# Adding slots on VectorE before TensorE sums them, in every group of a graph network kernel

## The reference, cut to what matters

```python
N_NODES, E, D = 6250, 200000, 16        # edges sorted by dst
w_m = (efeat @ W_msg + b_msg).reshape(E, 16, 16)
w_a = (efeat @ W_attn + b_attn).reshape(E, 16, 16)
h_src = feat[src][:, :, None]
e1, e2 = w_m * h_src, w_a * h_src
ex = exp(e2 - segment_max(e2, dst)[dst])
attn = ex / segment_sum(ex, dst)[dst]
ft = segment_sum(e1 * attn, dst).sum(axis=1)
x = layernorm(x + ft)
x = layernorm(x + segment_sum(edge_attr, dst) / max(counts, 1))
```

## Time and profile before

| | us |
|---|---|
| median of 3 runs | 2246.91 (2246.26 to 2247.14) |
| span of the profiled execution | 2950.2 |
| PE busy in it | 2137.9 |
| DVE busy | 1862.0 |
| POOL busy | 1687.5 |
| ACT busy | 1256.9 |
| mean granted TensorE clock | 0.861 |

### The profile page before, as it was taken

The page is one execution under the profiler, slowest core; times in us unless marked ns, Lnnn a source line. Parts: engine busy times, 40 slices in busy tenths (PEclk is TensorE's granted clock), DMA queues, the critical chain, the costliest instruction groups (busy, mean ns, idle before and its releaser), DMA issues. The chain is left out here.

```text
span 2950.2 us, 21765 instructions
## 1 busy us (share of the span) xinstructions
PE 2137.9 (72%) x6682; PEld 952.6 (32%) x6682; DVE 1862.0 (63%) x2907; ACT 1256.9 (43%) x1228; POOL 1687.5 (57%) x1845
## 2 busy tenths in 40 slices
PE   2347676676877777877787658877787767887777
PEld 1213233232333333333333223333333323333333
DVE  6246465566666666666676547766667656786776
ACT  3223443434444443454454325444444444554444
POOL 6556355665655565555565465655656565655633
PEclk8658888897988888989888889988989888988988
DMA  6000000000000000000000000000000001001000
GB/s 229 16 10 11 8 12 10 10 10 9 10 9 9 14 10 9 10 14 10 10 13 9 9 10 13 10 12 9 10 12 9 12 9 28 12 8 16 8 2 3
DMA packets 60073, 47.60 MB, mean 16 GB/s; under 512 B 28366, under 2 KB 55439, under 8 KB 59436
## 3 DMA queue, kind: packets, MB, share of 16 engines
q0 software_dynamic: 57632, 29.73, 8.0%
q1 hardware_dynamic: 2316, 16.38, 1.5%
HBM read 44.00 MB, written 1.90 MB: 16 GB/s over the span
## 5 line engine op out<-in xcount | busy, mean ns | idle before, releaser
L652 POOL DMA_INDIRECT AR<-in_xt,AR x1607 | 1538.8, 958 | 974.1 <-DVE AR L1472 491.3
L1128 PE MATMUL PX<-AR,CS 128*128 128x512 f32 x3246 | 1663.7, 642 | 37.8 <-issue 23.9
L1472 DVE CUSTOM_DVE_ANT_1 AR<-PW,AR 128x1024 f32<-128x1024 f32 x815 | 979.6, 1221 | 896.8 <-remote 651.2
L1108 PE MATMUL PW<-WS,LT 100*128 100x512 bf16 x1630 | 549.1, 423 | 683.9 <-DVE AR L1472 511.8
L1128 PEld LDWEIGHTS PX<-AR,CS 128*128 128x128 f32 x3246 | 664.9, 206 | 652.1 <-issue 532.4
L888 ACT ACTIVATE LT<-PTB 100x1024 bf16<-100x1024 bf16 (+1 forms) x221 | 211.2, 956 | 1005.7 <-remote 601.0
L1485 DVE TENSOR_TENSOR AR<-AR,PX 128x1024 f32<-128x1024 f32 (+1 forms) x442 | 501.0, 1134 | 121.3 <-ACT PX L944 76.0
L1108 PEld LDWEIGHTS PW<-WS,LT 100*128 100x128 bf16 x1630 | 141.5, 103 | 1113.7 <-DVE AR L1472 543.2
L946 ACT ACTIVATE AR<-AR 128x2048 f32<-128x2048 f32 (+1 forms) x221 | 412.9, 1869 | 7.2
L950 ACT ACTIVATE PX<-AR 128x1024 f32<-128x1024 f32 (+1 forms) x221 | 212.4, 961 | 412.3 <-DVE AR L1485 294.8
L944 ACT ACTIVATE PX<-AR 128x1024 f32<-128x1024 f32 (+1 forms) x221 | 231.0, 1045 | 39.4 <-DVE AR L1485 30.1
(11 more groups left out here) (192 smaller groups left out, 517.7 us busy)
## 6 DMA issues: line engine op xcount, KB each, us to landing
AR<-in_xt,AR POOLq DMA_INDIRECT x1607
AR<-in_eat SPq DMA_DIRECT2D x3, 3128.0 KB
AR<-in_eat SPq DMA_DIRECT2D x1, 3120.0 KB
y_d<-AR SPq DMA_DIRECT2D x1, 784.0 KB
AR<-y_d SPq DMA_DIRECT2D x1, 784.0 KB
AR<-in_es,E0I POOLq DMA_INDIRECT x48
y_d<-AR POOLq DMA_INDIRECT x36
CS<-in_cst SPq DMA_DIRECT2D x1, 442.0 KB, 5.3
```

What stands on the lines that cost most here:

```text
L652: g.indirect_dma_start(feat(h, j - j0, j - j0 + 1), None, xt, bass.IndirectOffsetOnAxis(ap=node, axis=0)).then_inc(hg_sem(h), 16)
L1108: i = pe.matmul(PAIRS[s % 2][:, j, :], LT[:, g % 3, lo:lo + 128], WS[:, :], start=True, stop=True)
L1128: i = pe.matmul(PDR, IDN, x, start=(a == 0 and j == 0), stop=(g == LAST[k] and j == n - 1))
L1472: v.tensor_tensor_reduce(em(g, j, j + 2).rearrange("p (x c) -> p x c", c=32), w, hb, 1.0, LOW, ALU.mult, ALU.max, accum_out=MXC[:, k % 2, ...
```

## The change

The list of groups whose slots VectorE adds first becomes all 221 groups:

```diff
 NORMS = [p for p, c in STEPS].index(FIRST[MAIN + 4] + 2)
-ADDS = [c for p, c in STEPS[-8:] if p is None]
+ADDS = list(range(NGR))
```

## The result

The changed kernel takes 2323.28 us (2322.32 to 2325.28, four runs), the kernel before 2246.59 (2244.28 to 2247.14, four runs): the ratio is 1.035, with a 95% interval of 1.0335 to 1.0364. The forecast was 2325.

What follows compares the result with a forecast made beforehand. GpSimd's gathers were taken as the bound: 2232 us plus 82 of holding gives 2314, against VectorE's 2255; with the leftover 2314 to 2329. Forecast 2325 us, 3.5% slower, range 2252 to 2352.

Steps and rivals of the forecast that it cites:

- The bound before: GpSimd's queue of gathers bounds the kernel before; its chain sums to 2232 us against the timed median of 2246.9.
- The missing 15 us: Part of the median before that GpSimd's sum left unexplained (0.7%); forecast to stay or shrink after the change.
- Part 1: TensorE sums fewer slots: 315 us less work, from 1843 to about 1528, off the path if GpSimd is the bound.
- Part 2: VectorE's new adds: 253 us more, 2025 us between first and last multiply; with 43 us for other waits, VectorE alone 2255.
- Part 4: Gathers starting inside an SBUF-and-SBUF add are held until it ends, less 0.12 us: 82 us more on GpSimd.
- lower bound of 46 us: Least price of the adds holding gathers, scaling the trace's 22 us of lengthening by add length and GpSimd's working share.
- The sum: GpSimd's chain 2232 + 82 = 2314 us against VectorE's 2255; with the leftover 2314 to 2329, forecast 2325, 3.5% slower.
- The first rival: Adds don't hold the gathers and VectorE is the bound: 2255 us (2225 to 2300); chance 0.17.
- The second rival: Timed runs are bound by TensorE handing pairs to VectorE, not by GpSimd: 2238 us; chance 0.06.
- The third: Gathers' hold-ups fall into GpSimd's waits for the ring, some 80 us free; VectorE still fits: 2247 us; chance 0.05.
- The fourth: Both effects plus a lower TensorE clock, VectorE and GpSimd waiting for each other: 2345 to 2380 us; chance 0.04.
- the signs listed: Gathers about 1000 ns or more, lengthened under L1493; 217 more adds; L1128 down a quarter; VectorE's L1108 waits shrink.

Runs made afterwards that it cites:

- b0_again: The kernel before, unchanged, run for a second trace because its first profiled span was 703 us too long: 2249.9 us (one run).
- b1: The kernel before with 213 of 1607 gathers left out (first slot of each group, columns 1 to 47): 2155.9 us, ratio 0.961.
- p1: The kernel before, all gathers, TensorE summing six of eight (five of six) slots, no new VectorE adds: 2245.5 us, ratio 1.0011.
- c2: The changed kernel with 213 gathers left out and TensorE still summing all slots, VectorE's adds kept: 2303.7 us, ratio 1.0238.
- p2: The changed kernel, all gathers and all adds, TensorE still summing all eight (six) slots: 2315.6 us, ratio 1.0323.
- a1: The changed kernel with 213 of 1607 gathers left out: 2305.8 us, ratio 1.0278 to the kernel before.
- h1: The changed kernel with the add in only every second group and the last four, all gathers: 2283.9 us, ratio 1.0158.
- h2: As the half-of-the-groups kernel, but its new adds replaced by a tensor_scalar with one SBUF input, 936 or 424 elements: 2250.2 us, ratio 1.0005.
- a2: The changed kernel with the 217 new adds replaced by a tensor_scalar with one SBUF input: 2321.2 us, ratio 1.0343.

## Why the prediction was right, and where it wasn't

**The bound before: right.** The forecast took GpSimd's gathers as the bound from a sum (2232 us), against a trace in which they weren't. b0_again shows VectorE waiting for gathers and never the other way, b1 gains 87 us by leaving gathers out, p1 gains nothing from a lighter TensorE. Setting the unnamed waits of the earlier trace rows aside, and adding up durations and spacings, was the right way to read a disturbed trace. The sum had one error that hid another: in undisturbed runs the steady gathers start at 73.8 us, not at 91.6, and the stretch behind the last gather is longer than 58 us. In b0_again the last gather starts at 2166.98, where the sum had 2174, and the end is 81 us later:

```profile
2166.98 0.94 POOL L652 DMA_INDIRECT AR<-in_xt,AR  x1 [0.30 <-issue]
```

The missing 15 us that the forecast carried along lie there: from the last gather to the last weights multiply it is 27 us, where the sum had 8. VectorE had fallen behind the gathers in the last columns, where it no longer waits for them.

**Part 1, TensorE's relief: right that it is off the path.** Its size was not: TensorE was to fall by 315 us and fell from 1965.8 to 1770.8, by 195. The same records got longer:

```profile
L1128 PE MATMUL PX<-AR,CS 128*128 128x512 f32 x3246 | 1553.5, 605 | 6.5 <-ACT AR L894 6.3
```

```profile
L1128 PE MATMUL PX<-AR,CS 128*128 128x512 f32 x2514 | 1306.2, 645 | 2.3 <-ACT AR L894 2.3
```

(before, second trace, then after: 605 and 645 ns). The mean granted clock went from 0.949 to 0.895. One place in the changed kernel where both show, TensorE and then VectorE:

```profile
331.15 0.60 PE L1108 MATMUL PW<-WS,LT 100*128 100x512 bf16 x2
334.95 1.03 PE L1108 MATMUL PW<-WS,LT 100*128 100x512 bf16 x2 [3.21 <-DVE AR L1472]
335.78 3.62 PE L1128 MATMUL PX<-AR,CS 128*128 128x512 f32 x4
339.19 1.06 PE L1108 MATMUL PW<-WS,LT 100*128 100x512 bf16 x2
```

```profile
338.23 0.08 DVE L1472 DVE_READ_ACCUMULATOR2_ANT AR<- 128x1 f32 x1
340.29 1.23 DVE L1472 CUSTOM_DVE_ANT_1 AR<-PW,AR 128x1024 f32<-128x1024 f32 x1 [1.98 <-PE PW L1108]
```

TensorE waits 3.21 us for VectorE (a product over the column's data, L1448, and the division and reduction, L1504 to L1506, stand before its next multiply) and comes back at a lower granted clock: 0.97 of full from 327.0 to 331.7 us, 0.88 from there to 334.95 and 0.50 from 334.95 to 339.2. Its weights product takes 1.03 us there, where the last one before the wait took 0.60. Its two slots then take 3.4 us until the next product, where they took 1.72 in the earlier trace rows, and VectorE stands for 1.98 us. So VectorE, though the bound, keeps losing time to the engine that waits for it. With a busier TensorE, in c2 and p2 (86% of the span in both, against 77% in a1 and 76% in the changed kernel), its mean clock is 0.950 and 0.946 (against 0.900 and 0.895) and the time is 0.1 to 0.4% better although it has more to do. What VectorE waits for before its weights multiplies is the same in sum, a1 then c2:

```profile
L1472 DVE CUSTOM_DVE_ANT_1 AR<-PW,AR 128x1024 f32<-128x1024 f32 x815 | 969.6, 1218 | 94.8 <-PE PW L1108 90.8 <-PE PX L1128 2.8 <-issue 0.4
...
L1473 DVE CUSTOM_DVE_ANT_1 AR<-PW,AR 128x1024 f32<-128x1024 f32 x815 | 969.1, 1219 | 93.3 <-PE PW L1109 66.7 <-issue 15.5 <-PE PX L1129 10.1
```

So less work at a lower clock and more work at a higher one hold VectorE up equally. What the clock costs by itself no run shows, since none changes the one without the other.

**Part 2, VectorE's work: the term that was mis-sized.** The forecast gave VectorE alone 2255 us. a1 measures 2306. The adds were right: 253 us forecast; measured were 215 more busy (1761 to 1976 between first and last multiply) and 23 of waiting right before them. The start was 22 us earlier than the disturbed trace had it. What failed is the idle time beside them, which I put at 64 us (21 for ScalarE, and 43, between 13 and 88, for TensorE's part and the filling). In a1 it is 185 us; less the 23 just named, 162. The waits for TensorE's products are the largest part, 91 us, then come 53 for ScalarE's exponentials before L1485, where the forecast had 21:

```profile
DVE AR L1472 <- PE PW L1108: 90.8, 75, 4.7
```

I had reasoned that these waits go away with TensorE's work, and they mostly don't: 113 us before (second trace), 84 with the change. Counted whatever the trace names as their end, VectorE's waits before its weights multiplies go from 151 us in b1 to 95 in a1, where the forecast left at most 88 and took 43.

**Part 4, the holding: right in mechanism, nearly twice too large, and not what set the time.** Gathers that start inside the add are held until it ends, less 0.12 to 0.13 us, by the rule that was read from two rows. Summed over the 178 gathers that begin inside an add it is 55 us (59 with the nine edge loads that do), against 82 forecast. Over all gathers it is 1607 x (0.985 - 0.960) = 40 us, since the operations that were there before hold the gathers for 9 us in sum, where they held them for 23 in b0_again. That lies under the forecast's lower bound of 46 us, which was itself added up wrongly: 22 x 230 / 162 / 0.77 is 41. With the edge loads, 4 us longer in sum, the last gather starts 45 us later than before:

```profile
2211.59 0.94 POOL L652 DMA_INDIRECT AR<-in_xt,AR  x1 [0.30 <-issue]
```

Where the gathers bind this costs its full price (34 us in h1 against h2). In the full change it costs 4 to 11 us by the estimate above, because GpSimd's chain, at an estimated 2247 + 45 = 2292 us, then lies below VectorE's level.

**The sum: right number, for a reason half wrong, so partly luck.** 2325 forecast, 2323 measured. The forecast had one chain at 2314 to 2329 and VectorE 60 us below it. In truth they are at 2292 (an estimate) and 2306 (a1), the other way round: the holding was put 37 us too high and VectorE's level 51 us too low, and that the number still came out is in part chance. The time comes out 17 us above the upper one. The changed kernel's trace has 29 us of waits for gathers up to 430 us (a1 has 9 there), none from there to 1593 us, and 13 more up to 1796, so gathers bind in some columns and VectorE in most; that this makes the 17 us fits, but no run shows it. The first rival (VectorE is the bound) had the right engine, but its number was worse (its range ended at 2300, and VectorE alone takes 2306), and its other half, that the adds don't hold the gathers, is false. The second rival falls with c2 and p1, since TensorE's relief is worth nothing as soon as either gathers or adds are there. The third falls with h1: the slack that it needs isn't there. The fourth named rightly that the clock falls (0.949 to 0.895; its remark that the dips follow idle time holds for the trace of before, where TensorE was idle for 50% of the 6.8 us ahead of a drop of the clock from full to half, the mean of the 90 drops of the steady work, against 26% over that whole stretch) and that VectorE and GpSimd wait for each other, but the time is not the 20 to 55 us above the forecast that it was given.

Of the signs listed: lengthened gathers under L1493, yes, at 985 ns and not 1000; 217 more instructions of 1.23 and 0.69 us, yes; L1128's count down by a quarter, yes, its time by a sixth; VectorE's waits on L1108 shrink, only from 113 to 84 us.

## What to carry to other kernels

Add up each engine's work and its own spacing before moving work from one engine to another, and against the median of timed runs, not the span of a disturbed trace: here TensorE was the busiest on both pages of the kernel before, and its relief was worth 98 us only when both the gathers and the adds were out of the way, nothing with either. Work moved to an engine at 85% did not just fill the remaining 15% here: most of the engine's idle time stayed, 185 us of 248, since it still waited for others (91 us for TensorE's products, 53 for ScalarE's exponentials). A tensor_tensor of VectorE with two SBUF inputs beside a full queue of indirect gathers had a second price here, paid by GpSimd: gathers of 977 ns on average in h1 against 958 in h2, and 34 us of time. The form with one input avoided it (958 ns), and so did an operand in PSUM (no gather over 0.97 us inside L1485 in the changed kernel).

## What the runs showed of the hardware

The added tensor_tensor of VectorE, with both inputs in SBUF, held an indirect gather that started on GpSimd while it was under way until the end of the operation less 0.12 to 0.13 us, if it had begun more than 0.04 us before the gather (165 of 178 gathers in the changed kernel's trace; a 0.94 us gather became 1.92). With one input in PSUM it didn't: in the same trace 344 gathers start inside such an operation of L1485, more than 0.12 us before its end, and in none with two SBUF inputs, and the longest takes 0.97 us. Nor did a tensor_scalar with an accumulated sum (mean gathers of 956 and 958 ns in a2 and h2, against 985 and 977 with the adds). TensorE's lighter load came with a lower clock: its f32 products of 512 columns took 605 ns on average at 87% busy and a granted clock of 0.949, and 645 ns at 76% and 0.895, so that TensorE's busy time fell by 195 us where its work fell by 315.
